# Score tiles in row-half pairs, one output block for both head groups, and longer score operands in a four-layer attention kernel

## What is computed

```python
def block0(x):   # 8 heads of 16, group norm over 16 groups
    xn = group_norm(x)
    q, k, v = split(xn @ w_qkv)             # per head: [1024, 16]
    p = softmax(q @ k.T * 16 ** -0.5)       # per head: [1024, 1024]
    return (p @ v) @ w_out + b_out + x
def block1(x):   # 8 heads of 16, group norm over 32 groups, q/k/v biases
    ...          # as above, but the sum is taken with xn and not with x
def block2(x):   # one head of 128, layer norm
    ...
def block3(x):   # one head of 128, group norm over 32 groups
    ...
```

## Time and profile before

| what | value |
|---|---|
| median of three runs | 2756.16 us |
| the profiled execution's own time | 2752.47 us |
| its span, first to last instruction | 2750.4 us |
| mean granted TensorE clock (share of 2.4 GHz) | 0.909 |
| TensorE matmul / weight load busy | 2525.4 / 1163.4 us |
| VectorE / ScalarE / GpSimd busy | 1729.6 / 1537.7 / 226.8 us |
| DMA | 96.81 MB, mean 35 GB/s |

### The profile page before, as it was taken

The page is one execution under the profiler, slowest core; times in us unless marked ns, Lnnn a source line. Parts: engine busy times, 40 slices in busy tenths (PEclk is TensorE's granted clock), DMA queues, the critical chain, the costliest instruction groups (busy, mean ns, idle before and its releaser), DMA issues.

```text
span 2750.4 us, 32645 instructions
## 1 busy us (share of the span) xinstructions
PE 2525.4 (92%) x12332; PEld 1163.4 (42%) x12332; DVE 1729.6 (63%) x3245; ACT 1537.7 (56%) x2009; POOL 226.8 (8%) x182
## 2 busy tenths in 40 slices
PE   4899899999999998999989999899998999999999
PEld 2333233333353335533354334543345433543666
DVE  2687566777858775676656766567665774554332
ACT  2266544665647664476644765357643776357554
POOL 3001010101000100001000010101000010000000
PEclk7589865888999999999999989998999999999999
DMA  7301340314040402204040040401304022000000
GB/s 142 47 1 26 60 70 8 64 22 78 1 77 10 72 6 41 45 9 78 1 77 16 3 78 8 70 17 30 49 16 66 5 38 41 1 9 1 5 5 16
DMA packets 53482, 96.81 MB, mean 35 GB/s; under 512 B 6736, under 2 KB 9424, under 8 KB 53200
## 3 DMA queue, kind: packets, MB, share of 16 engines
q1 hardware_dynamic: 53328, 94.74, 19.5%
HBM read 55.91 MB, written 37.75 MB: 34 GB/s over the span
## 4 chain that ended last, share of the span: by engine, by line
PE 76%; DVE 16%; ACT 3%; issue 3%; DMA 2%; SPq 1%; POOL 0%; ACTq 0%; DVEq 0%
PE outs L1126 18%; PE work L1081 15%; PE pairs L1103 9%; DVE part_max L907 9%; PE pairs L1139 9%; PE outs L1157 9%; PE work L1013 5%; PE work L1057 4%; PE work L1062 2%; DVE neg_max L931 2%; PE work L1053 2%; ACT probs L785 2%; PE outs L1166 1%; DVE o_turn L917 1%; DVE stats L838 1%
## 5 line engine op out<-in xcount | busy, mean ns | idle before, releaser
L907 DVE TENSOR_REDUCE part_max<-work 128x1 f32<-128x512 f32 x2048 | 1302.9, 681 | 579.1 <-PE work L1081 577.0
L785 ACT ACTIVATE probs<-pairs 128x1024 f32<-128x1024 f32 x1024 | 1005.0, 1023 | 386.4 <-PE pairs L1103 350.4
L1081 PE MATMUL work<-k_stack,q_stack 48*128 48x512 f32 x2048 | 748.2, 505 | 97.6 <-DVE part_max L907 68.9
L1103 PE MATMUL pairs<-q_stack,k_stack 50*128 50x512 f32 x2048 | 608.8, 480 | 32.8 <-ACT probs L785 23.5
L1081 PEld LDWEIGHTS work<-k_stack,q_stack 48*128 48x128 f32 x2048 | 323.2, 204 | 741.1 <-DVE part_max L907 350.7
L1126 PE MATMUL outs<-probs,v_heads 128*32 128x512 f32 x4096 | 611.9, 673 | 0.0
L1103 PEld LDWEIGHTS pairs<-q_stack,k_stack 50*128 50x128 f32 x2048 | 262.4, 202 | 205.9 <-ACT probs L785 119.4
L791 ACT ACTIVATE probs<-pairs,neg_max 128x1024 f32<-128x1024 f32 x128 | 142.7, 1115 | 346.0 <-DVE neg_max L931 346.0
L931 DVE TENSOR_REDUCE neg_max<-pairs 128x1 f32<-128x1024 f32 x128 | 156.7, 1224 | 175.0 <-PE pairs L1139 175.0
L1139 PE MATMUL pairs<-k_full,q_full 128*128 128x512 f32 x512 | 261.1, 634 | 0.0
L1157 PE MATMUL outs<-probs,v_full 128*128 128x256 f32 x1024 | 243.7, 392 | 0.7 <-DVE y L952 0.7
(11 more groups left out here) (80 smaller groups left out, 1095.8 us busy)
## 6 DMA issues: line engine op xcount, KB each, us to landing
k_stack<-k_scratch SPq DMA_DIRECT2D x96, 256.0 KB, 8.8
q_stack<-q_scratch SPq DMA_DIRECT2D x96, 256.0 KB, 8.7
k_scratch<-parts SPq DMA_DIRECT2D x32, 512.0 KB, 2.8
q_scratch<-parts SPq DMA_DIRECT2D x32, 512.0 KB, 13.0
q_stack<-shift_parts SPq DMA_DIRECT2D x256, 4.0 KB
tmp<-x SPq DMA_DIRECT2D x7, 512.0 KB, 3.4
out<-y SPq DMA_DIRECT2D x14, 256.0 KB, 2.0
w<-weights SPq DMA_DIRECT2D x1, 1152.0 KB, 7.3
```

The source lines that it names most:

```text
L785: nc.scalar.activation(probs[:, plan.prob[u], 2 * n:2 * n + 2, :], pairs[:, n, :, :], ACT.Exp, scale=HEAD_SCALE).then_inc(exp_done, 1)
L907: nc.vector.tensor_reduce(part_max[:, r % 2, column:column + 1], bank_of(("tile", r, n)), AX_X, ALU.max, negate=True).then_inc(tile_max, 1)
L1081: nc.tensor.matmul(bank_of(("tile", r, n)), qs[rows, i, a, heads, P * t:P * (t + 1)], ks[rows, i, keys, heads, :], start=True, stop=True). ...
L1103: last = nc.tensor.matmul(pairs[:, n, half, :], ks[rows, i, key // QT, first + n, P * (key % QT):P * (key % QT + 1)], qs[rows, i, a, first ...
```

## The change

1. **Tiles in pairs.** The planner counts pairs of tiles (2n, 2n+1), one in each row half, and always emits both together (`tile_pairs`, `take`). `beat` places the first pair, at most one chunk of TensorE, the second "pair" item, the values, and the rest. At the edges of full blocks a few items are interleaved differently.
2. **Shared output blocks.** GpSimd scales 16 of 32 columns into `o_both`, heads 0 to 3 in the first 16 and heads 4 to 7 in the last 16 of each block. One transpose back per half of a stage, one output matmul per chunk. Four DMAs ("merge") fill the gaps of the output weights with those of the other group.
3. **Longer operands for scores.** The shift rows move to the end of the row half, so tiles use 62 rows and "pair" 64. The rows between are zeros in `q_stack` (new memsets on VectorE) and ones in `k_stack`.
4. **Stacks read as 48 rows.** Each half is written three times, in the order of the stack (3 DMAs of 256 KB), and read with two DMAs of 48 rows.
5. **Placement.** From image 4 on, projections go to every second slot (`step` = 2), as do those of layer 1 of the last image and of layers 2 and 3 (those in pairs of chunks or packed into one beat aside). Image 1 is projected in the first slots and not ahead of them. `STACK_SLOTS` falls from 15 to 11. The code can split a chunk in two "pieces", but no piece is placed: projections stay whole.

```diff
-    FIRST_TILES = 40
+    FIRST_PAIRS = 20
...
+            if i == 1:
+                self.project(h(0, 1), 0, i, one)
             if i >= 2:
-                before = g0 - 2
-                at = h(before, {2: 16, 3: 21, 4: 21}.get(i, 10))
+                at = h(g0 - 2, {2: 16, 3: 23, 4: 18}.get(i, 14))
                 put(at - 3, ("load", i))
-                self.chain(at, 0, i, ["in0", "in1", *NORM])
-                self.project(h(g0 - 1, 1), 0, i, one)
+                at = self.chain(at, 0, i, ["in0", "in1", "stats", "gn1", "gn2"])
+                self.chain(at + (1 if i == 4 else 0), 0, i, ["apply"])
+                self.project(h(g0 - 1, 1), 0, i, one, 1 if i < 4 else 2)
...
-    STACK_SLOTS = 15
+    STACK_SLOTS = 11
...
+    def tile_pairs(self, b):
+        groups = []
         for r, n in self.tiles.get(b, []):
-            order.append(("tile", r, n))
-            if n == 2 and r > 0 and ("shift", r - 1) not in self.shifted:
-                order.append(("shift", r - 1))
-                self.shifted.add(order[-1])
+            groups.append([("tile", r, 2 * n), ("tile", r, 2 * n + 1)])
+            if n == 1 and r > 0 and ("shift", r - 1) not in self.shifted:
+                groups[-1].append(("shift", r - 1))
+                self.shifted.add(groups[-1][-1])
...
+            order = [("pair", 2 * n)] if own else []
+            order += take(1)
+            middle = [e for e in extra if self.on_tensor_engine(e)][:1]
+            order += middle
+            if own:
                 order.append(("pair", 2 * n + 1))
...
-            if s == 3 and r > 0 and not self.follows_full(n - 3):
+            if s == 3 and r % 4 in (3, 0) and r > 0 and not self.follows_full(n - 3):
                 order.append(("back", r - 1))
-            order += tiles[2:] + extra
+            order += take(len(groups)) + [e for e in extra if e not in middle]
...
-                    to = scratch[n][:, HEADS * half:HEADS * (half + 1), :, :]
-                    sp.dma_start(to.rearrange("j h r t -> (h r) j t"), parts[:, at, :, :].bitcast(F32)
-                                 ).then_inc(parts_out[at], 16)
+                    for b, part in enumerate(K_PART if n == "k" else Q_PART):
+                        to = scratch[n][b, :, half, :, :].rearrange("r h t -> h r t")
+                        sp.dma_start(to, parts[:, at, part, :].bitcast(F32)).then_inc(parts_out[at], 16)
...
+                    for half in range(2):
+                        rows = to[ROWS * half:ROWS * half + STACK, g % 2, :, :, :].rearrange("r a m t -> r (a m) t")
+                        heads = scratch[n].rearrange("b r a (m h) t -> h (b r) (a m) t", h=2)
+                        sp.dma_start(rows.bitcast(F32), heads[half]).then_inc(stacked[n], 16)
...
-                            at = ROWS * half + STACK + j
+                            at = ROWS * (half + 1) - SHIFT + j
...
                 def scale_outputs(r):
+                    g, half = r // 2 % 2, r % 2
                     pool.wait_ge(o_inverse, r + 1)
-                    inv = o_inv[:, r % 2, :].unsqueeze(2).to_broadcast([P, HALF // 32, 32])
-                    nc.gpsimd.tensor_tensor(o_turn[:, r % 2, :, :], o_turn[:, r % 2, :, :], inv,
+                    if r >= ROUNDS_OF_STAGE:
+                        pool.wait_ge(o_ready, 2 * (r // ROUNDS_OF_STAGE - 1) + half + 1)
+                    inv = o_inv[:, r % 2, :].unsqueeze(2).to_broadcast([P, HALF // 32, HD])
+                    nc.gpsimd.tensor_tensor(o_both[:, half, :, HD * g:HD * (g + 1)], o_turn[:, r % 2, :, 0:HD], inv,
                                             ALU.mult).then_inc(o_scaled, 1)
...
+                def zeros(half):
+                    first = ROWS * half + ROWS // 2
+                    nc.vector.memset(q_stack[first:first + ROWS // 2, :].bitcast(F32), 0.0).then_inc(zeros_ready, 1)
...
-                        for g in range(2):
-                            last = nc.tensor.matmul(bank, w_out(layer, g), oT[:, g, cols],
-                                                    start=g == 0, stop=g == 1)
+                        for j in steps:
+                            last = columns(j, w_out(layer), oT)
...
-                    rows = slice(ROWS * half, ROWS * half + STACK)
+                    rows = slice(ROWS * half, ROWS * (half + 1) - SHIFT)
...
-                        rows = slice(ROWS * half, ROWS * half + STACK + SHIFT)
+                        rows = slice(ROWS * half, ROWS * (half + 1))
```

More of the change, by code:

```diff
@@ L228, in place_tiles @@
         counts = [int(d + 1e-6) for d in done]
-        return {b: tiles[counts[b]:counts[b + 1]] for b in range(ends)}
-    STACK_SLOTS = 15
+        at = {b: pairs[counts[b]:counts[b + 1]] for b in range(ends)}
+        at[-1] = pairs[:self.FIRST_PAIRS]
+        return at
+    STACK_SLOTS = 11
     FULL_BEAT_WEIGHT = 1.6
@@ L267, in beat, with take @@
-        before = self.beats[b - 1][0] if b else None
-        after = self.beats[b + 1] if b + 1 < len(self.beats) else (None, None)
+        groups, extra = self.tile_pairs(b), self.extra.get(b, [])
+        kinds = [self.beats[a][0] if 0 <= a < len(self.beats) else None for a in range(b - 2, b + 3)]
+        def take(count):
+            taken = sum(groups[:count], [])
+            del groups[:count]
+            return taken
         if kind == "head":
             r, s = n // KT, n % KT
-            order = [] if before == "full" else [("pair", 2 * n)]
-            order += tiles[0:2]
-            if before != "full":
+            first, second = kinds[1] == "full", kinds[0] == "full" and kinds[1] == "head"
+            own = not first and not second
+            order = [("pair", 2 * n)] if own else []
[3 more added lines that the diff above has]
+            if own:
@@ L274, in beat @@
                 order.append(("pair", 2 * n + 1))
-            if before == "full":
+            if first:
                 order.append(("proj", self.beats[b - 1][1] // 2))
@@ L289, in beat @@
-        near = last or b + 2 >= len(self.beats) or self.beats[b + 2][0] != "full"
-        order = [("turn", n, 0), ("turn", n, 1), *tiles[0:1]]
-        if not near:
-            order.append(("scores", n + 2))
-        elif b + 2 < len(self.beats):
-            u = after[1] if last else self.beats[b + 2][1]
-            order.append(("pair", 2 * u + (1 if last else 0)))
-        order += tiles[1:3]
-        m = n // 2
-        if n % 2 == 0 and before == "full":
-            order += [("pv", m - 1, k) for k in range(KT)]
-        elif n % 2 and self.beats[b - 2][0] == "full":
-            order.insert(2, ("proj", m - 1))
@@ L302, in beat @@
-        order += tiles[3:] + extra
-        if last and after[0] is not None:
-            order += self.full_end(n, False)
-        return order
+            order += take(len(groups)) + [e for e in extra if e not in middle]
+            if kinds[3] == "full":
+                m = self.beats[b + 1][1]
+                order += [("scores", m), ("values", n), ("outputs", r), ("scores", m + 1)]
+                groups.extend(self.tile_pairs(b + 1))
+                order += take(len(groups) - 1) + [("back", r)] + take(1)
@@ new lines, in beat @@
+            return order
+        if kinds[1] == "head":
+            groups = []
+        order = [("turn", n, 0), ("turn", n, 1)]
+        m = n // 2
+        if n % 2 and kinds[0] == "full":
+            order.append(("proj", m - 1))
+        order += take(1)
+        if kinds[4] == "full":
+            order.append(("scores", n + 2))
+        elif "head" in kinds[3:]:
+            u = self.beats[b + (1 if kinds[3] == "head" else 2)][1]
+            order.append(("pair", 2 * u + (1 if kinds[3] == "head" else 0)))
@@ new lines, in beat, with on_tensor_engine @@
+        order += take(1)
+        if n % 2 == 0 and kinds[1] == "full":
+            order += [("pv", m - 1, k) for k in range(KT)]
+        order += take(len(groups)) + extra
+        if kinds[3] == "head":
+            u = self.beats[b + 2][1]
+            order += [("pv", m, k) for k in range(QT)] + [("pair", 2 * u)]
+            order += [("pv", m, k) for k in range(QT, KT)] + [("pair", 2 * u + 1)]
+        return order
+    def on_tensor_engine(self, item):
+        return item[0] == "piece" or item[0] == "chunk" and item[1] not in NO_BANK
@@ L309, in follows_full @@
         return b > 0 and self.beats[b - 1][0] == "full"
-    def full_end(self, n, end):
-        m = n // 2
-        return [*[("pv", m, k) for k in range(KT)], *([("proj", m)] if end else [])]
     def count(self):
```

199 lines of the change are left out of this document (113 added, 86 removed).

## The result

The changed kernel takes 2762.05 us (median of 20 runs), the kernel before 2772.59 (median of 20 on the same chip). The ratio of the two is 1.0075, 95% interval 1.004 to 1.011; like all ratios here it leaves out the slower runs of the kernel before and so lies above the ratio of the medians, 0.996. Either way it is no gain, where 2596 us was forecast. The profiled execution of the changed kernel took 2772.2 us, span 2770.1.

What follows compares the result with a forecast made beforehand. TensorE, busy 2525 of 2750 us, was taken as the bound, with 500 us at 1.2 GHz. Terms -33, -5, -40, -6, -76 and 0 took 2752.5 to 2592.5, plus 3.7 gave 2596 us; range 2480 to 2710.

Steps and rivals of the forecast that it cites:

- Tiles in pairs: Score tiles on TensorE: 458 fewer separate stretches, 197 us of TensorE time, one fifth taken: -40 us, ends -150 and +60.
- under 600: Sign in the score tiles: TensorE busy below 600 us on them, with 2048 instructions.
- The start: Start of the kernel: idle time, stack writes and reads, image 1's work and zeroing sum to -6 us, ends -20 and +8.
- before 85: Sign at the start: the first exponential's scores come before 85 us, where they came at 92.9.
- The zeroing: New q_stack zeroing on VectorE at the start: 7 us, twice; the first delays the statistics, +1.6 us.
- The clock: TensorE's clock level: fuller rows and packed pairs raise it sooner, -76 us, ends 0 and -153.
- The first rival: TensorE's clock does not follow the added zero rows, so its term is 0: 2672 us, chance 0.25.
- Output projections: Output matmuls on TensorE: one per half instead of two, 64 instructions fewer, -33 us, ends -33 and -15.
- the turning back: Transposes back on VectorE fall from 64 to 32: -5 us, ends 0 and -22.
- Every second slot: Projections spread over twice the slots, stacks called ready after 11 slots instead of 15: 0 us, ends -15 and +15.
- The second rival: Pairs in head rounds wait for a second work bank, one more maximum each: +120 us, 2876 us, chance 0.05.

Runs made afterwards that it cites:

- e10_chunk_last: The changed kernel with all chunks at the slot's end, none between the first pair of tiles and the second exponential's scores; 2662.58 us.
- e9: e2_rows_out with tiles in pairs and the changed order of a slot, old stacks and old placement kept; 2766.97 us.
- e15: e10_chunk_last with the stacks and the placement of the kernel before; 2640.81 us.
- e16: The kernel before with a slot's first work-bank chunk moved between its first two tiles and the second exponential's scores; 2900.39 us.
- e5_all_single: The changed kernel without the pairs and the new order inside a slot, tiles single and ordered as before; 2689.60 us.
- e2_rows_out: The kernel before with longer score operands and the shared output block; 2656.14 us.
- e3_rows_out_stack: e2_rows_out with each stack half written in three DMAs and read as 48 rows; 2689.77 us.
- e1_rows: The kernel before with only the score operands lengthened, to 62 and 64 rows filled with zeros; 2676.79 us.
- e17_last_rows48: e10_chunk_last with the tiles back on 48 rows and "pair" on 50; 2755.78 us.
- e14: e10_chunk_last with the stacks written and read as before the change; 2628.71 us.

## Where the prediction was right and where it failed

**The step that failed is "Tiles in pairs", -40 us.** It priced what a pair saves and what a second bank costs, and took the order around it as given. The change's own order puts up to one chunk for each slot between the first pair of tiles and the second "pair" item, and the prediction gave that no price, though it wrote that "what queues behind that wait is the exponentials' scores and the values product, and ScalarE behind them". The measured price is 100 us (e10_chunk_last), 126 (e9 to e15) and 138 (alone, e16), with such a chunk in 208, 213 and 219 slots. The pairs themselves did pay: 27 us between e5_all_single and e10_chunk_last by the medians and 1.9% by the ratios, 15 us and 0.5%, from different batches and so within the error, between e2_rows_out and e15_last_oldstacks_place. Against these, one fifth of 197 us of TensorE time was a guess of the right order, if a high one, and a fraction picked without a row behind it. The packing itself fell short: L1152 is busy 676 us, not under 600, and 676.0 / 0.481 = 1405 separate stretches are left of 1482, where 1024 were counted on. With the chunk the step is worth +72 us, beyond its upper end of +60.

**The start failed as well, -6 with ends -20 and +8.** It was not run alone as a whole, but its stacks cost +34 us (e3_rows_out_stack), some 18 to 21 of it in the first round. The term sized the reads by how many partitions they use, and the writes by their bytes at the 233 GB/s of the earlier trace rows. That figure is the mean of a stretch with the DMA engines 60% busy (the reads' row beside it says 129 GB/s, not 128); the old writes run at 397 while they run, the new ones at 205. From first issue to release of the read 1.5 MB in six writes took 11.3 us, 139 GB/s. The step had the reads' gain at -8 and the writes' loss at +2; the gain is about -2 (0.6 for q, 1.4 for k), the loss 6.8 for k's writes alone, with q's behind them. By the port rule of the Trainium skill, "SBUF — State Buffer", section "Door 1: The DMA port swizzle", the prediction estimated reads up to twice as fast; no such gain shows in this case, 13.6 to 13.0 us, though the old reads are six short ones in flight together and so no clean test of the rule. The first exponential's scores came at 96.3 us, not before 85; the idle time before them did fall from 7.49 to 2.34 us, but everything ahead was later. The changed kernel's start:

```profile
7.01 6.88 DVE L1003 MEMSET q_stack<- 32x8192 f32 x1 [1.76 <-issue]
13.92 1.29 DVE L881 BATCH_NORM_STATS2 stats<-x 128x6 f32<-128x512 f32 x2
...
69.52 1.19 PE L1152 MATMUL work<-k_stack,q_stack 62*128 62x512 f32 x3 [29.66 <-issue]
...
96.32 0.80 PE L1174 MATMUL pairs<-q_stack,k_stack 64*128 64x512 f32 x2 [2.34 <-DMA q_stack<-shift_parts]
```

The zeroing's own row has 6.88 us, near the 7 worked out. But VectorE stands for another 1.76 us before it with nothing that it waits for, before the second zeroing as well, so that from the end of the instruction before (5.25) to the next (13.92) the zeroing cost 8.67 us. The prediction scaled the row of L970 alone and left out the 0.4 us of idle time that the earlier trace rows shows with it. The statistics move from 8.23 to 13.92 us, 5.7 us where 4.4 were seen; the first projection comes 3 us later, not 1.6.

**The clock was right, in cause and in size.** -76 was forecast; the rows alone gave 82 us by the medians and 74 by the ratio (e1_rows), 93 us and 4.3% when undone (e17_last_rows48), and the lower-level time fell by 233 us in e1_rows, (1 - 0.950) x 2 x 2675 = 267 left of 500. 233 x 0.34 is 79, so the price of 0.34 holds. The sum is right in part by luck: from 300 to 400 us, where -10 was forecast, the mean clock is 0.73 in e1_rows as it was 0.74 before, and the stretches from 100 to 200 us (0.71 to 0.99) and from 400 to 500 us (0.52 to 1.00) give the most. The first rival is out. It was the reading by the Trainium skill, "TensorE: Matmul & The Clock Gate", section "What's actually happening": the gate goes by how busy TensorE is. The trace disagrees again, with 95.39 of 95.60 us busy at 1.2 GHz in e17_last_rows48, and a higher level in e1_rows with TensorE less busy.

**Output projections**: -33 forecast, 21 measured together with the turning back (-5), inside the ends -15 and -33. The transposes went to 32 and TensorE saved 31 us.

**Every second slot**: 0 forecast, 0 measured (e3 against e5; 12 us, within the error, between e14 and e15). Both comparisons also hold the move of image 1's projections, which the start term had at -7.5, +6 and so nearly nothing.

**The second rival** (a second bank as the wait) had the sign of the loss right and the wrong cause. The idle time before the tiles rose from 420 to 535 us, which the prediction would have read as this rival. But it stays at 349 + 86 = 436 us in e10_chunk_last, which has the same pairs and is 100 us faster, and shorter maxima made the wait the same in both orders and closed 15 of 72 us. A wait that grows on the engine's way is no proof that it is the cause.

By the medians the parts of the change are -82 (rows), -21 (outputs), +34 (stacks), 0 (placement), -27 (pairs) and +100 (the chunk in the middle), together +4.

## What to carry to other kernels

When a list orders several engines, price every item that moves by what stands behind it in each engine's queue, not by its own duration: here a projection of about 1.1 us, moved ahead of a slot's second scores, made ScalarE start its second exponential 2.1 us after the first, and such chunks in 208 slots cost the kernel 100 us, some 0.5 us each. A change of several parts needs its parts timed alone: gains of 130 us were in this one, and moving one chunk and taking one part back gives 2628.71 us, 0.956 of the kernel before. For transfers, time the writes that a reader's nicer layout demands before believing in the faster reads.

## What the runs showed of the hardware

- Rows filled with zeros count for the clock: tiles on 62 instead of 48 rows and scores on 64 instead of 50 took the mean granted clock from 0.909 to 0.950 and 82 us off by the medians, with the same products summed.
- One write of 128 partitions and 512 KB replaced by three of 256 KB, two halves of k each: 11.3 us from the first issue to the release of the read, against 4.5 for the 1 MB of before. Both count: half as many bytes again, and 205 GB/s with the DMA engines 0.53 busy against 397 GB/s at 1.03. Which part of the new pattern halves the rate was not tried.
- A 48-row read of 1.5 MB took 13.0 us, three 16-row reads for each half 13.6.
- VectorE's zeroing of 32 x 8192 float32 elements took 6.88 us by its row and 8.67 us from the end of the instruction before to the next.
